# Regrouping the fetch of edge slots in a graph layer, and moving its evictions and splits between two engines

## The chip, the cores and the metric

One core of one Trainium2 chip runs the whole kernel as one program. The metric is the device time in microseconds (us) of one execution, and the time of a kernel is the median over several executions.

## The reference

The kernel computes two rounds of message passing with a gated recurrent cell, on 12,500 nodes with 64 features and 400,000 edges. The edges come sorted by `dst`; the sum goes by `src` (the reference names it `row`).

```python
h = jnp.maximum(_layernorm(x, axis=-1), 0.0)
for t in range(2):
    m_input = jnp.concatenate([h[dst], h[src], edge_weight1], axis=1)
    messages = m_input @ msg_W[t].T + msg_b[t]
    agg = jax.ops.segment_sum(messages, src, num_segments=12500)
    h = _gru_cell(agg, h, gru_Wih[t], gru_bih[t], gru_Whh[t], gru_bhh[t])
return x + h
```

## The kernel before, in words

The nodes lie in 98 tiles of 128 (`NT`). The edges are cut into 112 windows (`C`), one to a partition, 3572 edges each. The program goes through four parts.

1. Loading and packing, to about 100 us. Each edge is packed into two 32-bit words that hold the source node, the place of the destination in its window, and the bits of the edge's weight (`attr`).
2. A sort of each window's words by source tile, to about 600 us. VectorE (DVE in the profile) does the merge steps, ScalarE (ACT) copies, layer norm and counts beside them.
3. The spreading block (lines 831 to 950), from 600 to about 719 us. For each window and each node tile it takes the 64 slots in which the edges of that tile lie. It is the part that the change rewrites.
4. Two rounds (`sums_round`, line 969), 720 to 1563 us and 1574 to 2399 us. TensorE (PE) gathers rows of `h` with one-hot matrices from VectorE, ScalarE evicts them, TensorE scatters them into sums per node, and the gate arithmetic follows two tiles behind.

The spreading block goes by groups of tiles, given by the table `GROUPS` at line 787: tiles 0 to 23, 24 to 47, 48 to 71 and 72 to 97.

- SyncE stores the sorted words to memory (L834). Then GpSimd (POOL) issues 49 indirect fetches (L848), each for a pair of tiles, into `taken`. They are all in one queue and wait for nothing but the sorted words. Each group has a semaphore of its own, `taken_in[g]`.
- VectorE waits for its group (L903) and decodes it in seven passes, one after the other: the lane of the destination (L920), the source tile's place (L922 and L927 or L929), the two pieces of the weight (L930, L931, L933), and their sum (L934, which raises `src_ready`). All seven cover the 112 windows and all slots of the group: 64 elements for each tile. Where the group crosses the middle of the tiles (`MID`), the subtraction is in two instructions. In the last group a check of the slots' ends comes first (L908 to L914).
- TensorE turns the decoded slots, four tiles to a pack (L862 for the source lanes, L863 for the weights), into two banks each of PSUM, so that pack k waits until pack k-2 has been evicted.
- ScalarE evicts the source lanes (L881, two halves of each pack) into `src_lane`, and VectorE evicts the weights (L941) into `attr_slot`.
- At the end of a group the weights are split into a 16-bit high part and a 16-bit rest scaled by 2048: ScalarE makes the high part (L888), VectorE subtracts it (L945), ScalarE scales the rest (L890) and writes the high part beside it (L892). VectorE's next group comes behind L945.
- ScalarE also converts the destination lanes (L874), which SyncE stores to memory (L838) for the rounds.
- After the last group come a short check (L947, L948, L868, L950), whose result `misfit` every engine reads before the rounds.

At the start of a round VectorE clears two small buffers (L1346, L1349) and the whole of `rows` (L1351); in round 0 it then writes ones into one column (L1354). Only then comes its first one-hot matrix (L1284), which needs the lanes that were fetched from memory (L1017, issued by GpSimd in round 0 and by SyncE in round 1). TensorE and ScalarE wait for `rows_zero` before their first instruction of a round. In round 0 a row of `rows` has 132 elements of 16 bits: 128 features that ScalarE writes (L1200), two that VectorE writes (L1289), the ones, and a last one. In round 1 it has 128, all written by ScalarE.

Of the kernel before, what the change touches and what calls it, by code (L numbers as in the profile page):

```python
# [130 lines left out]
def build(nc, x, src, dst, attr, msg_W, msg_b, Wih, bih, Whh, bhh, out):  # L131
    N, H = x.shape
    E = src.shape[0]
    ROUNDS = msg_W.shape[0]
    NT = -(-N // P)
# [3 lines left out]
    C = 112  # L139
# [6 lines left out]
    J = -(-C // 2)  # L146
# [22 lines left out]
    with ExitStack() as ctx:  # L169
# [12 lines left out]
        def sem(name):  # L182
            return ctx.enter_context(nc.semaphore(name))
# [3 lines left out]
        def path_sem(name):  # L187


            if name not in path_sems:  # L190
                path_sems[name] = sem(name)
            return path_sems[name]
# [19 lines left out]
        h = sb("h", [P, NT, HA])  # L212
# [574 lines left out]
        GROUPS = [range(4 * (a * -(-NT // 4) // 4), min(4 * ((a + 1) * -(-NT // 4) // 4), NT)) for a in range(4)]  # L787
# [33 lines left out]
        high_cut = sem("high_cut")  # L821
        low_left = sem("low_left")
        low_cut = sem("low_cut")
# [7 lines left out]
        with nc.Block() as block:  # L831
# [39 lines left out]
            def _(act):  # L871
                for g, group in enumerate(GROUPS):
# [12 lines left out]
                    at = slice(group[0], group[-1] + 1)  # L885
                    act.wait_ge(attr_kept, 2 * (group[-1] // 4 + 1))
                    wait(act, low_left, g)
                    nc.scalar.activation(attr_high[:, 0:len(group), :], attr_slot[:, at, :], ACT.Copy).then_inc(high_cut, 1)  # L888
                    act.wait_ge(low_left, g + 1)
                    nc.scalar.activation(attr_two[:, at, :, 1], attr_slot[:, at, :], ACT.Copy, scale=LO).then_inc(low_cut, 1)  # L890
                    act.wait_ge(low_cut, g + 1)
                    nc.scalar.activation(attr_two[:, at, :, 0], attr_high[:, 0:len(group), :], ACT.Copy)  # L892

            @block.vector
            def _(dve):
# [5 lines left out]
                for g, group in enumerate(GROUPS):  # L901
# [34 lines left out]
                    for k, pack in enumerate(PACKS):  # L936
                        if pack[0] not in group:
                            continue
                        dve.wait_ge(slots_ps, k + 1)
                        for half in range(2):  # L940
                            nc.vector.tensor_copy(attr_slot[half * SLOTS:(half + 1) * SLOTS, pack[0]:pack[-1] + 1, :],  # L941
                                                  ps_attr[k % 2][0:SLOTS, 0:len(pack) * C]
                                                  .rearrange("p (s j h) -> p s j h", j=J, h=2)[:, :, :, half]).then_inc(attr_kept, 1)
                    dve.wait_ge(high_cut, g + 1)
                    nc.vector.tensor_tensor(attr_slot[:, at, :], attr_slot[:, at, :], attr_high[:, 0:n, :], ALU.subtract).then_inc(low_left, 1)  # L945
# [23 lines left out]
        def sums_round(r, scope):  # L969
# [18 lines left out]
            else:  # L988
# [13 lines left out]
             rz_ready, tn_ready, cand_ready, mixed, h_new, ones_ready, joined_ready) = [path_sem(f"{n}_{r}") if more or n not in ("attr_sum", "ones_ready") else None for n in names]  # L1002
# [22 lines left out]
            with nc.Block() as block:  # L1025
# [87 lines left out]
                def _(te):  # L1113
# [57 lines left out]
                    te.wait_ge(rows_zero, 1)  # L1171
# [22 lines left out]
                def _(act):  # L1194
# [46 lines left out]
                    act.wait_ge(rows_zero, 1)  # L1241
# [37 lines left out]
                def _(dve):  # L1279
# [71 lines left out]
                    nc.vector.memset(rows[:], 0.0).then_inc(rows_zero, 1)  # L1351
                    if r == 0:
                        dve.wait_ge(rows_zero, 1)
                        nc.vector.memset(rows[:, :, :, 2 * H + 2:2 * H + 3], 1.0).then_inc(ones_ready, 1)  # L1354
                        dve.wait_ge(ones_ready, 1)
# [297 lines left out]
```

## Time and profile before

| what | value |
|---|---|
| runs | 2413.81 us median of 3 (2413.45 to 2416.66) |
| the profiled execution's own time | 2400.32 us |
| its span, first to last instruction | 2398.8 us |
| spreading block and start of round 0 | 599.84 to 725.12 us |
| VectorE busy | 2192.0 us, 91% |
| ScalarE busy | 1963.7 us, 82% |
| TensorE busy | 1621.8 us, 68%; granted clock 0.979 |
| GpSimd busy | 612.9 us, 26% |

The span runs from the first to the last instruction of the profiled execution, and its own time is 1.5 us longer. Times of rows are in microseconds from the start of the span. A row of the timeline gives start, duration, engine, line, operation, output and inputs, and in brackets how long the engine had been idle before it and what ended that. Consecutive instructions of the same kind are merged into one row (x2, x4). Busy times do not say what bounds a stretch; for that the waits at each place are read.

### The profile page before, as it was taken

What the parts mean: (1) busy time and instruction counts of PE and PEld (TensorE: products, weight loads), DVE (VectorE), ACT (ScalarE), POOL (GpSimd) and SP (SyncE); (2) the same over time, 40 slices, a digit from 0 to 9 for tenths busy, and PEclk for the clock granted to TensorE, in tenths of its full rate; (3) what the DMA queues carried; (4) which work ended last, traced back from release to release, by engine and by line L of the source; (5) the groups of instructions that cost most, each with busy time, mean ns of one, the idle gap of its engine ahead of it and who ended that gap; (6) DMA issues with size and microseconds to landing.
All of it is one profiled execution on the core that took longest, in us unless ns stands there. A gap on an engine that the chain in (4) does not pass through costs nothing. (4 is left out here: it accounts for less than half of the span.)

```text
span 2398.8 us, 126601 instructions
## 1 busy us (share of the span) xinstructions
PE 1621.8 (68%) x47260; PEld 1529.0 (64%) x47260; DVE 2192.0 (91%) x3766; ACT 1963.7 (82%) x4390; POOL 612.9 (26%) x853
## 2 busy tenths in 40 slices
PE   0000000000138899999999999968999999999996
PEld 0000000000138899999999999858999999999996
DVE  6999999999369899999999999868999999999995
ACT  3776895563158899999999999868999999999996
POOL 1000000000633344454554444401211111211121
PEclk9999999999968999999999999989999999999998
DMA  5100001110426666666666666556766777677773
GB/s 105 41 0 0 0 0 38 45 22 21 124 49 228 211 226 224 232 228 227 227 228 227 226 231 225 176 193 202 238 235 233 243 233 239 235 243 233 237 237 116
DMA packets 175418, 400.70 MB, mean 167 GB/s; under 512 B 73071, under 2 KB 76789, under 8 KB 174855
## 3 DMA queue, kind: packets, MB, share of 16 engines
q1 hardware_dynamic: 116907, 204.17, 27.0%
q0 software_dynamic: 57296, 195.19, 24.4%
q8 instruction: 49, 0.80, 0.1%
q10 hardware_dynamic: 1132, 0.27, 0.1%
q14 instruction: 34, 0.28, 0.0%
HBM read 384.63 MB, written 14.57 MB: 166 GB/s over the span
## 5 line engine op out<-in xcount | busy, mean ns | idle before, releaser
L1200 ACT ACTIVATE rows<-ps_rows 128x512 f16<-128x512 f32 x2744 | 1454.4, 637 | 66.9 <-PE ps_rows L1123 44.3
L1140 PE MATMUL ps_sum<-rows,src 128*64 128x132 f16 (+1 forms) x21952 | 1153.3, 225 | 15.0 <-ACT rows L1200 9.4
L1140 PEld LDWEIGHTS ps_sum<-rows,src 128*64 128x64 f16 x21952 | 905.1, 142 | 26.8 <-ACT rows L1200 18.6
L1293 DVE TENSOR_TENSOR src<-iota_units,src_lane 128x2048 f16<-128x2048 f16 (+1 forms) x784 | 863.3, 1101 | 42.7 <-PE ps_sum L1140 42.6
L1123 PE MATMUL ps_rows<-rows_next,dst 128*64 128x128 f16 x10976 | 547.9, 220 | 37.2 <-DVE dst L1284 22.3
L1123 PE MATMUL ps_rows<-rows_now,dst 128*64 128x128 f16 x10976 | 546.1, 220 | 22.2 <-DVE dst L1284 10.3
L1284 DVE TENSOR_SCALAR dst<-lanes,lane_no 128x2048 f16<-128x2048 f16 (+1 forms) x784 | 533.0, 680 | 4.2 <-DMA lanes<-lanes_dram 3.6
L862 PE MATMUL ps_src<-ident,late 112*64 112x112 f32 x98 | 29.9, 337 | 627.0 <-DVE taken L934 626.4
L1123 PEld LDWEIGHTS ps_rows<-rows_next,dst 128*64 128x64 f16 x10976 | 413.0, 111 | 60.4 <-issue 26.9
L1123 PEld LDWEIGHTS ps_rows<-rows_now,dst 128*64 128x64 f16 x10976 | 412.9, 111 | 45.3 <-issue 15.9
L862 PEld LDWEIGHTS ps_src<-ident,late 112*64 112x64 f32 x98 | 14.6, 149 | 629.7 <-DVE taken L934 627.3
L1017 POOL DMA_DIRECT2D lanes<-lanes_dram x392 | 242.5, 619 | 467.5 <-DVE dst L1284 400.9
L1052 POOL COPY copied<-h 128x64 f32 (+1 forms) x196 | 173.5, 886 | 606.3 <-PE ps_T L1155 596.9
L848 POOL DMA_INDIRECT taken<-sorted_dram,start_i x49 | 58.3, 1189 | 571.7 <-DMA sorted_dram<-planes 557.1
L291 ACT ACTIVATE beyond<-src_i,below 128x3572 bf16<-128x3572 int32 x49 | 159.7, 3260 | 24.4 <-issue 20.2
L1165 PE MATMUL ps_gates<-w_first,turned_now 128*64 128x256 f32 x784 | 119.6, 381 | 5.9 <-ACT turned_now L1214 3.3
L1167 PE MATMUL ps_gates<-w_second,turned_now 128*64 128x256 f32 x784 | 118.9, 379 | 0.0
L1214 ACT ACTIVATE turned_now<-ps_T 128x256 f32<-128x256 f32 x196 | 77.6, 396 | 4.9 <-PE ps_T L1155 4.9
L1289 DVE COPY rows<-attr_room 128x32 f16 (+3 forms) x392 | 74.1, 189 | 7.7 <-PE ps_sum L1140 7.6
L1153 PE MATMUL ps_T<-ident,copied 128*64 128x128 f32 x392 | 76.2, 276 | 0.0
L1152 PE MATMUL ps_T<-ident,joined 128*64 128x128 f32 x392 | 76.1, 276 | 0.0
L1167 PEld LDWEIGHTS ps_gates<-w_second,turned_now 128*64 128x64 f32 x784 | 57.6, 137 | 27.2
(188 smaller groups left out, 2052.6 us busy)
## 6 DMA issues: line engine op xcount, KB each, us to landing
lanes<-lanes_dram POOLq DMA_DIRECT2D x294, 512.0 KB, 4.8
lanes<-lanes_dram SPq DMA_DIRECT2D x294, 512.0 KB, 4.7
lanes<-lanes_dram POOLq DMA_DIRECT2D x98, 256.0 KB, 4.1
lanes<-lanes_dram SPq DMA_DIRECT2D x98, 256.0 KB, 4.1
rows_now<-parts_dram SPq DMA_DIRECT2D x112, 32.0 KB, 1.7
rows_next<-parts_dram SPq DMA_DIRECT2D x112, 32.0 KB, 3.6
parts_dram<-rows_now SPq DMA_DIRECT2D x1, 3136.0 KB, 16.2
sorted_dram<-planes SPq DMA_DIRECT2D x1, 3136.0 KB, 11.6
```

What stands on the lines that cost most here:

```text
L291: nc.scalar.activation(beyond[:], src_i[:], ACT.Sign, bias=below[:, m:m + 1], accum_out=balance[:, m:m + 1]).then_inc(counts_ready, 1)
L1017: plain(engine.dma_start(lanes[q][:, 0:n * SLOTS], lanes_dram[bass.ds(s, 1), q * QC * SLOTS:(q * QC + n) * SLOTS] .broadcast_to([P, n * SL ...
L1052: plain(nc.gpsimd.tensor_copy(copied[b][:], h[:, bass.ds(k, 1), 0:H].rearrange("p o f -> p (o f)"))).then_inc(copied_ready, 1)
L1123: last = nc.tensor.matmul(ps_rows[(u + NU * b) % 4][half * SLOTS:(half + 1) * SLOTS, k * 2 * H:(k + 1) * 2 * H], dst1[q][:, (c - q * QC) * ...
L1140: last = nc.tensor.matmul(ps_sum[b][at, 0:width], hot[:, at], row, start=(j == 0), stop=(j == J - 1))
L1153: nc.tensor.matmul(ps_T[high, 0:P], copied[b][:], ident[:], start=True, stop=True)
L1165: nc.tensor.matmul(ps_gates[at, to], turned_now[b][:, at], w_first[:, r, :], start=True, stop=False)
L1167: last = nc.tensor.matmul(ps_gates[at, to], turned_now[b][:, P + at.start:P + at.stop], w_second[:, r, :], start=False, stop=True)
L1200: nc.scalar.activation(rows[:, (u + NU * b) % ring, 0:n, 0:2 * H], cut(ps_rows[(u + NU * b) % 4][:])[:, 0:n, :], ACT.Copy).then_inc(rows_r ...
L1214: nc.scalar.activation(turned_now[b][:], ps_T[:, 0:2 * P], ACT.Copy).then_inc(T_ready, 1)
L1284: nc.vector.tensor_scalar(dst1[q][:, 0:n * SLOTS], lanes[q][:, 0:n * SLOTS], lane_no[:, 0:1], None, ALU.is_equal).then_inc(dst1_ready, 1)
L1293: nc.vector.tensor_tensor(src1[q][:, 0:len(units)], iota_units[:].rearrange("p (o l) k -> p o l k", o=1) .broadcast_to([P, len(units), P, ...
```

## The change

The groups become 32, 28, 20 and 18 tiles. ScalarE evicts both halves of a pack, source lanes and weights. The split of the weights is now four instructions of VectorE alone (L937 to L940 in the changed kernel), and it stands one group later: after the decode of group g+1 VectorE splits group g. In the rounds, only columns 130 and 131 of `rows` are zeroed in round 0, and nothing in round 1; the waits for `rows_zero` are left in round 0 alone.

```diff
-        GROUPS = [range(4 * (a * -(-NT // 4) // 4), min(4 * ((a + 1) * -(-NT // 4) // 4), NT)) for a in range(4)]
+        ENDS = [0, *(4 * (NT * part // (4 * 49)) for part in (16, 30, 40)), NT]
+        GROUPS = [range(ENDS[a], ENDS[a + 1]) for a in range(4)]
...
-                    at = slice(group[0], group[-1] + 1)
-                    act.wait_ge(attr_kept, 2 * (group[-1] // 4 + 1))
-                    wait(act, low_left, g)
-                    nc.scalar.activation(attr_high[:, 0:len(group), :], attr_slot[:, at, :], ACT.Copy).then_inc(high_cut, 1)
-                    act.wait_ge(low_left, g + 1)
-                    nc.scalar.activation(attr_two[:, at, :, 1], attr_slot[:, at, :], ACT.Copy, scale=LO).then_inc(low_cut, 1)
-                    act.wait_ge(low_cut, g + 1)
-                    nc.scalar.activation(attr_two[:, at, :, 0], attr_high[:, 0:len(group), :], ACT.Copy)
+                        for half in range(2):
+                            nc.scalar.activation(attr_slot[half * SLOTS:(half + 1) * SLOTS, pack[0]:pack[-1] + 1, :],
+                                                 ps_attr[k % 2][0:SLOTS, 0:len(pack) * C]
+                                                 .rearrange("p (s j h) -> p s j h", j=J, h=2)[:, :, :, half],
+                                                 ACT.Copy).then_inc(attr_kept, 1)
...
-                    for k, pack in enumerate(PACKS):
-                        if pack[0] not in group:
-                            continue
-                        dve.wait_ge(slots_ps, k + 1)
-                        for half in range(2):
-                            nc.vector.tensor_copy(attr_slot[half * SLOTS:(half + 1) * SLOTS, pack[0]:pack[-1] + 1, :],
...
-                    dve.wait_ge(high_cut, g + 1)
-                    nc.vector.tensor_tensor(attr_slot[:, at, :], attr_slot[:, at, :], attr_high[:, 0:n, :], ALU.subtract).then_inc(low_left, 1)
+                def split_attr(g):
+                    n, at = len(GROUPS[g]), slice(GROUPS[g][0], GROUPS[g][-1] + 1)
+                    dve.wait_ge(attr_kept, 2 * -(-(GROUPS[g][-1] + 1) // 4))
+                    step(nc.vector.tensor_copy(attr_high[:, 0:n, :], attr_slot[:, at, :]))
+                    step(nc.vector.tensor_tensor(attr_slot[:, at, :], attr_slot[:, at, :], attr_high[:, 0:n, :], ALU.subtract))
+                    step(nc.vector.tensor_scalar(attr_two[:, at, :, 1], attr_slot[:, at, :], LO, None, ALU.mult))
+                    step(nc.vector.tensor_copy(attr_two[:, at, :, 0], attr_high[:, 0:n, :]))
+
+                decode(0)
+                for g in range(1, len(GROUPS)):
+                    decode(g)
+                    split_attr(g - 1)
+                split_attr(len(GROUPS) - 1)
...
-                    te.wait_ge(rows_zero, 1)
+                    if r == 0:
+                        te.wait_ge(rows_zero, 1)
...
-                    nc.vector.memset(rows[:], 0.0).then_inc(rows_zero, 1)
                     if r == 0:
+                        nc.vector.memset(rows[:, :, :, 2 * H + 2:width], 0.0).then_inc(rows_zero, 1)
                         dve.wait_ge(rows_zero, 1)
```

`decode(g)` is the body of the old loop over the groups, from the wait for the fetch to L934.

The order on VectorE, at the end of one decode and through the next. Before, group 0 (`late` and `taken` are the decoded words, `ps_attr` the turned weights, `attr_room` holds `attr_slot` and `attr_two`):

```order
L927 TENSOR_TENSOR late<-tile_base,late 112x1536
L930 TENSOR_SCALAR taken<-taken 112x12x128
L931 TENSOR_SCALAR taken<-taken 112x12x128
L933 TENSOR_SCALAR taken<-taken,units 112x12x128
L934 SCALAR_TENSOR_TENSOR taken<-taken,units 112x12x128
L941 COPY attr_room<-ps_attr 64x224 x12
L945 TENSOR_TENSOR attr_room<-attr_room,late 128x1344
L920 TENSOR_SCALAR late<-taken 112x1536
```

With the change, from the end of the decode of group 0 to the split of its weights:

```order
L930 SCALAR_TENSOR_TENSOR taken<-taken,units 112x16x128
L916 TENSOR_SCALAR late<-taken 112x1792
L918 TENSOR_SCALAR late<-taken 112x1792
L923 TENSOR_TENSOR late<-tile_base,late 112x1152
L925 TENSOR_TENSOR late<-late,tile_base 112x640
L926 TENSOR_SCALAR taken<-taken 112x14x128
L927 TENSOR_SCALAR taken<-taken 112x14x128
L929 TENSOR_SCALAR taken<-taken,units 112x14x128
L930 SCALAR_TENSOR_TENSOR taken<-taken,units 112x14x128
L937 CAST late<-attr_room 128x1792
L938 TENSOR_TENSOR attr_room<-attr_room,late 128x1792
L939 TENSOR_SCALAR attr_room<-attr_room 128x1792
```

The evictions have left VectorE, the next decode follows at once, and the split of the older group comes behind it.

The same engine at the end of the block. Before:

```order
L934 SCALAR_TENSOR_TENSOR taken<-taken,units 112x13x128
L941 COPY attr_room<-ps_attr 64x224 x12
L941 COPY attr_room<-ps_attr 64x112 x2
L945 TENSOR_TENSOR attr_room<-attr_room,late 128x1456
L947 TENSOR_REDUCE over<-ps_check 6x1
```

With the change:

```order
L929 TENSOR_SCALAR taken<-taken,units 112x9x128
L930 SCALAR_TENSOR_TENSOR taken<-taken,units 112x9x128
L937 CAST late<-attr_room 128x1120
L938 TENSOR_TENSOR attr_room<-attr_room,late 128x1120
L939 TENSOR_SCALAR attr_room<-attr_room 128x1120
L940 COPY attr_room<-late 128x1120
L937 CAST late<-attr_room 128x1008
L938 TENSOR_TENSOR attr_room<-attr_room,late 128x1008
L939 TENSOR_SCALAR attr_room<-attr_room 128x1008
L940 COPY attr_room<-late 128x1008
L948 TENSOR_REDUCE over<-ps_check 6x1
```

Two splits stand behind the last decode now, that of group 2 and that of group 3, and the check behind them.

ScalarE in the last group. Before:

```order
L874 ACTIVATE planes<-late 112x1664
L881 ACTIVATE src_lane<-ps_src 64x224 x12
L881 ACTIVATE src_lane<-ps_src 64x112 x2
L888 ACTIVATE late<-attr_room 128x1456
L890 ACTIVATE attr_room<-attr_room 128x1456
L892 ACTIVATE attr_room<-late 128x1456
```

With the change:

```order
L872 ACTIVATE planes<-late 112x1152
L879 ACTIVATE src_lane<-ps_src 64x224 x2
L884 ACTIVATE attr_room<-ps_attr 64x224 x2
...
L879 ACTIVATE src_lane<-ps_src 64x112 x2
L884 ACTIVATE attr_room<-ps_attr 64x112 x2
L829 UNCONDITIONAL_BRANCH
```

ScalarE has four evictions for each pack, and nothing behind the last pack.

## Rows read from the trace of the kernel before

**Rows 1.** Timeline of VectorE, group 0.
```profile
629.74 0.96 DVE L920 TENSOR_SCALAR late<-taken 112x1536 int32<-112x1536 int32 x1 [29.20 <-DMA taken<-sorted_dram,start_i]
...
634.40 0.96 DVE L931 TENSOR_SCALAR taken<-taken 112x1536 int32<-112x1536 int32 x1
...
636.46 1.82 DVE L934 SCALAR_TENSOR_TENSOR taken<-taken,units 112x1536 f32<-112x1536 int32 x1
...
648.06 1.56 DVE L945 TENSOR_TENSOR attr_room<-attr_room,late 128x1344 f32<-128x1344 f32 x1 [1.39 <-ACT late L888]
```

**Rows 2.** Timeline of GpSimd: fetches; below, landing after their start, 684 to 685.
```profile
626.22 0.92 POOL L848 DMA_INDIRECT taken<-sorted_dram,start_i  x1 [0.30 <-issue]
...
629.90 1.78 POOL L848 DMA_INDIRECT taken<-sorted_dram,start_i  x1 [0.30 <-issue]
631.99 2.49 POOL L848 DMA_INDIRECT taken<-sorted_dram,start_i  x1 [0.30 <-issue]
...
636.84 2.23 POOL L848 DMA_INDIRECT taken<-sorted_dram,start_i  x1 [0.30 <-issue]
...
641.83 0.93 POOL L848 DMA_INDIRECT taken<-sorted_dram,start_i  x1 [0.30 <-issue]
...
684.41 0.93 POOL L848 DMA_INDIRECT taken<-sorted_dram,start_i  x1 [0.30 <-issue]
...
DMA to landing us min/median/max: 2.6/2.7/2.7
```

**Rows 3.** Timeline of VectorE, the last group and the check.
```profile
690.07 0.24 DVE L908 TENSOR_SCALAR planes<-taken 112x98 int32<-112x98 int32 x1
...
691.79 1.88 DVE L920 TENSOR_SCALAR late<-taken 112x1664 int32<-112x1664 int32 x1
...
697.42 1.09 DVE L930 TENSOR_SCALAR taken<-taken 112x1664 int32<-112x1664 int32 x1
...
713.44 1.67 DVE L945 TENSOR_TENSOR attr_room<-attr_room,late 128x1456 f32<-128x1456 f32 x1 [1.48 <-ACT late L888]
...
715.76 0.15 DVE L950 TENSOR_SCALAR misfit<-ps_check 1x1 int32<-1x1 f32 x1 [0.28 <-PE ps_check L868]
```

**Rows 4.** Timeline of TensorE, first turned tiles of groups 0 and 3.
```profile
638.33 0.39 PE L862 MATMUL ps_src<-ident,late 112*64 112x112 f32 x1 [585.09 <-DVE taken L934]
...
702.88 0.39 PE L862 MATMUL ps_src<-ident,late 112*64 112x112 f32 x1 [16.52 <-DVE taken L934]
```

**Rows 5.** Timeline of ScalarE, first eviction, four in a row, and the block's end.
```profile
640.07 0.72 ACT L881 ACTIVATE src_lane<-ps_src 64x224 f16<-64x224 f32 x2 [7.85 <-PE ps_attr L863]
...
664.08 1.49 ACT L881 ACTIVATE src_lane<-ps_src 64x224 f16<-64x224 f32 x4 [0.52 <-PE ps_attr L863]
...
716.99 1.82 ACT L892 ACTIVATE attr_room<-late 128x1456 f16<-128x1456 f16 x1
```

**Rows 6.** Groups by shape, a conversion while loading: busy us, mean ns, idle us before.
```profile
L413 DVE CAST iota_units<-src_lane 128x512 f16<-128x512 int32 x1 | 0.4, 421 | 0.0
```

**Rows 7.** Groups by shape, 629 to 716 us: evictions by VectorE.
```profile
L941 DVE COPY attr_room<-ps_attr 64x224 f32<-64x224 f32 x48 | 18.4, 383 | 16.1 <-PE ps_attr L863 15.0
```

**Rows 8.** Timeline and landing time of the first fetch of lanes, start of round 0.
```profile
720.14 0.19 DVE L1346 MEMSET extras<- 128x64 f32 x2 [4.24 <-issue]
...
720.51 2.22 POOL L1017 DMA_DIRECT2D lanes<-lanes_dram  x4 [35.17 <-issue]
721.32 3.14 DVE L1351 MEMSET rows<- 128x3696 uint32 x1 [0.85 <-DVE extras L1349]
725.12 0.75 DVE L1284 TENSOR_SCALAR dst<-lanes,lane_no 128x2048 f16<-128x2048 f16 x1 [0.29 <-DMA lanes<-lanes_dram]
...
DMA to landing us min/median/max: 4.5/4.5/4.5
```

**Rows 9.** Timeline of VectorE, start of round 1.
```profile
1574.50 0.91 DVE L1351 MEMSET rows<- 128x1024 uint32 x1 [0.30 <-DVE extras L1349]
1577.94 0.75 DVE L1284 TENSOR_SCALAR dst<-lanes,lane_no 128x2048 f16<-128x2048 f16 x1 [2.53 <-DMA lanes<-lanes_dram]
```

More of the change, by code:

```diff
@@ L820, in build @@
         attr_kept = sem("attr_kept")
-        high_cut = sem("high_cut")
-        low_left = sem("low_left")
-        low_cut = sem("low_cut")
         lanes_out = sem("lanes_out")
@@ L900, in _, with decode @@
                 step(nc.vector.tensor_copy(check[:, 1:5], stray[:]))
-                for g, group in enumerate(GROUPS):
+                def decode(g):
+                    group = GROUPS[g]
                     n, at = len(group), slice(group[0], group[-1] + 1)
@@ L935, in _ @@
                                                    op0=ALU.mult, op1=ALU.add).then_inc(src_ready, 1)
-                    for k, pack in enumerate(PACKS):
-                        if pack[0] not in group:
-                            continue
-                        dve.wait_ge(slots_ps, k + 1)
-                        for half in range(2):
-                            nc.vector.tensor_copy(attr_slot[half * SLOTS:(half + 1) * SLOTS, pack[0]:pack[-1] + 1, :],
-                                                  ps_attr[k % 2][0:SLOTS, 0:len(pack) * C]
-                                                  .rearrange("p (s j h) -> p s j h", j=J, h=2)[:, :, :, half]).then_inc(attr_kept, 1)
-                    dve.wait_ge(high_cut, g + 1)
-                    nc.vector.tensor_tensor(attr_slot[:, at, :], attr_slot[:, at, :], attr_high[:, 0:n, :], ALU.subtract).then_inc(low_left, 1)
+                def split_attr(g):
[10 more added lines that the diff above has]
+                split_attr(len(GROUPS) - 1)
                 dve.wait_ge(check_ps, 1)
@@ L1001, in sums_round @@
              extras_zero, extras_ready, scaled_ready, copied_ready, turned, T_ready, gates_ready,
-             rz_ready, tn_ready, cand_ready, mixed, h_new, ones_ready, joined_ready) = [path_sem(f"{n}_{r}") if more or n not in ("attr_sum", "ones_ready") else None for n in names]
+             rz_ready, tn_ready, cand_ready, mixed, h_new, ones_ready, joined_ready) = [path_sem(f"{n}_{r}") if more or n not in ("attr_sum", "ones_ready", "rows_zero") else None for n in names]
             lanes_in = [path_sem(f"lanes_in{r}_{q}") for q in range(NQ)]
@@ L1239, in tanhs @@
                         nc.scalar.activation(cand[:], tn[:], ACT.Tanh).then_inc(cand_ready, 1)
-                    act.wait_ge(rows_zero, 1)
+                    if r == 0:
+                        act.wait_ge(rows_zero, 1)
                     def body(s, b, half):
```

## The prediction

> **What bounds the kernel now.** I read the page first: VectorE is busiest, but the edit touches only 600 to 725 us and the start of each round, so shares over the whole span say nothing about it. The timelines of that stretch, engine by engine, do. In group 0 VectorE starts when its fetches have landed, decodes from 629.74 [rows 1] until TensorE starts at 638.33 [rows 4], 8.59 us, and evicts. It then waits 1.39 us for ScalarE and subtracts at 648.06 [rows 1]. The later groups follow directly: their fetches have landed by the time VectorE asks. The last fetch starts at 684.41 [rows 2], and VectorE opens the last group at 690.07 [rows 3]. So before, VectorE's chain with its two partners is the bound. The block ends with ScalarE's last copy, 716.99 + 1.82 = 718.81 [rows 5], and round 0 begins 1.33 us later, at 720.14 [rows 8].
>
> GpSimd is the second chain, 2 us in hand. Alone, a fetch takes 0.92 us and the next comes 1.23 us after it. In this decode fetches take 1.78, 2.49 and 2.23 us, under evictions out of PSUM again 0.93 [rows 2]. The slow ones end at joints of VectorE's work: the one from 631.99 ends at 634.48, where L931 starts at 634.40, and the one from 636.84 ends at 639.07, 0.79 us after the sum L934 ended at 638.28 [rows 1, 2]. A fetch passes two gates: its start waits behind any of the seven passes, its end only behind the passes at two elements a cycle.
>
> **The parts, priced.**
>
> *First group.* 16 fetches instead of 12. The 15th starts at 629.90, the 16th 1.23 later at 631.13; from start to VectorE takes 3.52 us (626.22 to 629.74) [rows 1, 2]: decode 0 starts at 634.65, 4.9 us later than before. The last fetches landed 2.7 us after their start [rows 2]; if those on which VectorE waits do too, each wait ends 0.75 us earlier, which I keep as a bound.
>
> *Decodes.* A pass at two elements a cycle costs 0.96 us for 1536 elements [rows 1] and 0.42 for 512 [rows 6]: 0.067 us for each pair of tiles (128 elements). At one a cycle it is 1.56 us for 1344, so 0.133 a pair. Five of one and two of the other make 0.60 a pair: 11.0 us for 16 pairs, 9.8 + 0.2 for 14 (the subtraction is in two), 7.4 for 10. The last group has 9 pairs, an odd number, and the nearest row is the old last group of 13. There L920 took 1.88 us where twelve pairs took 0.96, and L930 took 1.09 [rows 3]; the four slow passes lose 0.133 a pair, the three in place 0.27 altogether: 702.88 - 691.79 = 11.09 [rows 3, 4] less 2.1 less 0.8 is 8.2 us. The check ahead of it costs 1.72 (690.07 to 691.79). Were L920 slow for another reason than the odd count, the last decode would be 1.2 us cheaper.
>
> The Trainium skill says why the count should matter (VectorE: DVE Perf Modes, What auto-detection actually checks): two elements a cycle from one source need outermost dimensions of source and destination that are both even or equal. By that rule nine pairs are slow again in L916 and L918; without it the end is 1.2 us earlier.
>
> *Splits.* Not in the trace as VectorE work. Nearest: the conversion of 512 at 0.42 us [rows 6] and the subtraction [rows 1]. For 1792, 1568, 1120 and 1008 weights that gives 5.4, 4.9, 3.7 and 3.4 us; at one element a cycle for three of the passes the last would be 5.0. I take the first, since nothing here reads PSUM.
>
> *Evictions.* VectorE's took 383 ns [rows 7]; four on ScalarE are 1.49 us, 373 ns each [rows 5]. That is TensorE's own pace for a pack at the start of a group (640.07 + 1.49). So four and a half packs take 1.74 us to the first eviction, then 4 x 1.49 + 1.1, and 0.3 where TensorE waits for a bank: 9.1 us. If a 32-bit output costs more, 0.5 us for each 0.1 us a pack.
>
> [...]
>
> *The fetch queue.* This decides. I step the 33 remaining fetches along VectorE's new order by the two gates. Stepped so along the old order, they end within 1.3 us of the last row. While decode 0 runs (to 645.65), GpSimd gets through three and a half; alone again it ends the 30th at 656.4, and group 1 opens at 659.0. VectorE has idled 13 us there, since split 0 stands behind decode 1 and cannot fill it. Decode 1 and split 0 run to 674.4 and hold the fetches back again; the 40th ends at 676.6, group 2 opens at 679.2. Decode 2 and split 1 run to 691.5, the 49th fetch starts at 692.6, 8.2 us later than before, and group 3 opens at 696.1.
>
> *The tail.* 696.1 + 1.7 + 8.2 = 706.0. Split 2 lies beside the evictions, which end at 715.1. Split 3 ends at 718.5, the check takes 0.8 more (713.44 + 1.67 to 715.76 + 0.15 [rows 3]), and 1.33 later round 0 begins: 720.6 to 720.9, against 720.14. **Block: +0.6 us.** VectorE's chain loses its evictions, 12 x 0.38 = 4.6 us a group [rows 7] and the waits between them, and gets them back as waits for fetches.
>
> *The clearing.* It removes 3.14 us in round 0 and 0.91 in round 1. But lanes fetched at 720.51 land 4.5 us later, at 725.0, and VectorE's first one-hot starts at 725.12 [rows 8]: the clearing ended just as they landed. Without it VectorE waits for the lanes, worth 0.1 us; at most 0.3 more if the landing gets shorter. In round 1 VectorE waits 2.53 us for lanes after the clearing [rows 9]: nothing. TensorE and ScalarE wait for the one-hots anyway. **-0.1 us.**
>
> Sum: +0.5 us on the profiled execution's 2400.3. That execution is 0.6% under the median of the runs, so I carry the ratio: 2413.8 + 0.5 = **2414.3 us**. Bounds of the open prices: landing 0.75 earlier, the odd count 1.2 earlier, the gates 1 each way, new passes that hold no fetch 2 earlier, evictions and split 3 slower 2 to 3 later. They will not all fall on one side: -4 to +4 us.
>
> **Rivals.** About 0.2%, 4.8 us, is what a measurement of this kernel can tell from no change.
>
> 1. *The fetches are not held.* At 1.23 us each the last would start at 671.7, the decodes would come when VectorE is ready (decode 1 at 651.9, decode 2 at 667.3), the last would end near 689.6, and round 0 would begin near 704: 16 us less, 2398 us. For it: larger passes leave fewer joints but also fewer interruptions. Against it: all three rows under the decode are 1.78 or more [rows 2]. 8%.
> 2. *Slower: fetches miss the joints.* Passes follow within 0.04 us, and the splits lengthen the bursts behind decodes 1 and 2. If no fetch gets through under a split, four more fetches queue: 4 x 1.23 = 4.9 us later, 2419. If none gets through in any burst (11.0, 15.4 and 12.3 us), the last starts near 710, 18 us later, 2432. It decides from the fourth missed fetch on. Against it: four got through in each old decode. 10%.
> 3. *The clearing counts in full*: 4.0 us off, 2410, within 0.2%. Against it are the two waits for lanes. 4%.
> 4. *The same chain, cheaper*: splits at 32 bits or with 16-bit outputs do not hold the fetches (2 us) and the landing is early (0.75): 2411 to 2413. For it: no row shows a pass with a 16-bit output beside a fetch. Against it: the decode's passes of the same kind did. 12%.
>
> The Trainium skill (SBUF — State Buffer, Who interferes with whom) says that a VectorE instruction in a two-port mode shuts GpSimd out for the whole instruction, and one with two SBUF inputs only its reads. Of this change it says beware: the splits are put where fetches are issued. Taken instruction by instruction it gives my walk; taken for a whole burst, rival 2.
>
> **How the numbers follow.** The forecast holds 66%, rivals 4 and 3 fall within 0.2% too. Faster by over 0.2%: 8% and 1 for an unseen one, 9%. Slower: 10%. Within: 81%. The range 2409 to 2420 takes in the bounds and the near end of rival 2.
>
> **What would show it.** In the new trace: decode 0 opens near 634.7; VectorE idles some 13, 5 and 5 us ahead of decodes 1, 2 and 3, each ended by the fetch; the last fetch starts near 692.6; L916 takes about 1.35 us in the last group; split 3 starts about 9 us behind the last decode; round 0's first one-hot waits 3 to 4 us for lanes and starts near 725.6. If the last fetch starts before 688 or after 697, the walk is wrong; if decodes 1 to 3 open without idling, rival 1 is right; if one-hots start 2 us or more ahead of 725, rival 3.

## The result, and the profile after

| | kernel before | changed kernel |
|---|---|---|
| runs beside each other, median | 2413.63 us (8 runs, 2406.81 to 2420.17) | 2402.03 us (8 runs, 2394.16 to 2406.0) |
| profiled execution: its own time, span | 2400.32, 2398.8 us | 2394.16, 2392.5 us |
| granted TensorE clock, mean | 0.979 | 0.981 |
| ratio, 95% interval | | 0.9949 [0.9931, 0.9967] |

So the change is 0.5% faster, about 12 us, where no change was forecast (+0.5 us). The two profiled executions are only 6.2 us apart, half of that; where the rest lies turned out to be the lesson of this case.

The changed kernel's spans must be read with an offset. Its spreading stretch starts, at own_start, at 596.04 us; in the kernel before at 599.87. I call the time from own_start to round 0's first one-hot **the stretch**: 725.12 - 599.87 = 125.25 us before, 718.60 - 596.04 = 122.56 after. VectorE in the stretch, from the timeline of the changed kernel (start, us, engine, line, operation, in brackets the idle time before it and what ended it):

```profile
596.04 0.15 DVE L892 TENSOR_SCALAR own_start<-lane_no 128x1 f32<-128x1 f32 x1 [0.33 <-PEq L596]
...
630.16 1.23 DVE L916 TENSOR_SCALAR late<-taken 112x2048 int32<-112x2048 int32 x1 [33.44 <-DMA taken<-sorted_dram,start_i]
...
638.74 2.35 DVE L930 SCALAR_TENSOR_TENSOR taken<-taken,units 112x2048 f32<-112x2048 int32 x1
653.53 1.09 DVE L916 TENSOR_SCALAR late<-taken 112x1792 int32<-112x1792 int32 x1 [12.44 <-DMA taken<-sorted_dram,start_i]
...
663.38 1.09 DVE L937 CAST late<-attr_room 128x1792 f16<-128x1792 f32 x1
...
672.83 0.83 DVE L916 TENSOR_SCALAR late<-taken 112x1280 int32<-112x1280 int32 x1 [3.83 <-DMA taken<-sorted_dram,start_i]
...
689.17 0.25 DVE L904 TENSOR_SCALAR planes<-taken 112x98 int32<-112x98 int32 x1 [4.11 <-DMA taken<-sorted_dram,start_i]
...
690.90 1.34 DVE L916 TENSOR_SCALAR late<-taken 112x1152 int32<-112x1152 int32 x1
...
697.58 1.42 DVE L930 SCALAR_TENSOR_TENSOR taken<-taken,units 112x1152 f32<-112x1152 int32 x1
...
707.99 0.69 DVE L937 CAST late<-attr_room 128x1008 f16<-128x1008 f32 x1 [5.31 <-ACT attr_room L884]
...
713.92 0.18 DVE L1349 MEMSET extras<- 128x64 f32 x2 [1.58 <-issue]
...
718.60 0.75 DVE L1287 TENSOR_SCALAR dst<-lanes,lane_no 128x2048 f16<-128x2048 f16 x1 [3.75 <-DMA lanes<-lanes_dram]
```

The reader is to see the three new waits for the fetch, 12.44, 3.83 and 4.11 us, where VectorE had none [rows 3]; the last group, 689.17 to 699.00, in place of a decode of 13 pairs; split 3 waiting for ScalarE; and the one-hot waiting 3.75 us for its lanes where it started on time before [rows 8]. The fetches, from GpSimd's timeline of the changed kernel, the answer to [rows 2]:

```profile
627.36 0.93 POOL L846 DMA_INDIRECT taken<-sorted_dram,start_i  x1 [0.30 <-issue]
...
629.83 1.67 POOL L846 DMA_INDIRECT taken<-sorted_dram,start_i  x1 [0.30 <-issue]
631.81 1.52 POOL L846 DMA_INDIRECT taken<-sorted_dram,start_i  x1 [0.31 <-issue]
633.63 2.60 POOL L846 DMA_INDIRECT taken<-sorted_dram,start_i  x1 [0.30 <-issue]
```

The first of these is the 16th fetch, the other three are the 18th to the 20th. Alone a fetch takes 0.93 us; under decode 0 they are held, as forecast (a fetch is held when it takes longer because VectorE is at work). And VectorE opens at 630.16, 2.80 us after the start of the 16th fetch at 627.36, not 3.52.

ScalarE now evicts both kinds. Its timeline in group 0 of the changed kernel:

```profile
647.38 0.72 ACT L879 ACTIVATE src_lane<-ps_src 64x224 f16<-64x224 f32 x2
648.13 0.72 ACT L884 ACTIVATE attr_room<-ps_attr 64x224 f32<-64x224 f32 x2
650.64 0.72 ACT L879 ACTIVATE src_lane<-ps_src 64x224 f16<-64x224 f32 x2 [1.79 <-PE ps_attr L861]
...
656.31 0.72 ACT L879 ACTIVATE src_lane<-ps_src 64x224 f16<-64x224 f32 x2 [4.20 <-remote]
...
659.90 0.72 ACT L879 ACTIVATE src_lane<-ps_src 64x224 f16<-64x224 f32 x2 [2.12 <-PE ps_attr L861]
...
662.89 1.70 ACT L872 ACTIVATE planes<-late 112x1792 f16<-112x1792 int32 x1
```

The pace is 1.50 us a pack, as priced. But packs 5, 6 and 7 (650.64, 656.31, 659.90) come 1.8, 4.2 and 2.1 us late from TensorE, 8 us together. No row of the kernel before had such a gap, and I first took it for harmless: VectorE waits for fetches until 653.53, decode 1 needs no eviction, and split 0 asks for them only at 663.38, when they have just ended.

### The profile page after: what moved, and what is told of

Same layout as the page of the kernel before. It is cut to its first block and busy times, and to the rows that moved or that the text cites. A ratio compares the mean times of both kernels' runs of the same rounds, so it can differ in the third digit from the quotient of the medians.

```text
span 2392.5 us, 126600 instructions
## 1 busy us (share of the span) xinstructions
PE 1623.6 (68%) x47260; PEld 1526.9 (64%) x47260; DVE 2179.6 (91%) x3727; ACT 1963.7 (82%) x4428; POOL 616.3 (26%) x853
## 5 line engine op out<-in xcount | busy, mean ns | idle before, releaser
L846 POOL DMA_INDIRECT taken<-sorted_dram,start_i x49 | 63.8, 1302 | 571.7 <-DMA sorted_dram<-planes 557.1
## 6 DMA issues: line engine op xcount, KB each, us to landing
sorted_dram<-planes SPq DMA_DIRECT2D x1, 3136.0 KB, 11.6
```

## The experiments

Every series of executions ran the kernel before on the same chip beside the kernels under test. The single time of a program spreads by about 0.7%, so I read two numbers of each: the ratio, and the stretch in the trace. The walk, below, is the one of the prediction: the fetches stepped one after the other along VectorE's order of work.

**Repeats.** No edit: the kernel before and the changed kernel once more. Theories at this point: *A*, the edit gains on VectorE's chain in the stretch; *B*, chance or loading (the first VectorE operation that needs a bias, L433, started at 27.53 us against 31.38, which accounts for 3.85 of the 6.2 us).

> The kernel before, unchanged, timed against itself. It tells how far the ratio of two equal kernels strays, and gives a second trace of the old program. Theory A (the gain is what the two traces show between the start of the spreading block and the first one-hot, 125.25 against 122.56 us, and the rest is chance from execution to execution): ratio 1.000 within its interval, that stretch again 125.3 us within 0.5, while the weights' addition L433, which started at 31.38 us before and at 27.53 with the change, may start anywhere between. Theory B (the changed program as a whole is placed or loaded differently, and gains outside the stretch too): L433 again at 31.4 here.

> The changed kernel again, unchanged. Theory A: stretch from own_start to the first one-hot 122.6 us within 0.5, that is 2.7 us less than before, and a ratio of about 0.999; L433 anywhere between 27 and 32 us. Theory B: ratio again near 0.995, L433 again at 27.5 us.

Measured, in one series: before_twice 0.9996 [0.9979, 1.0014], stretch 124.79 us; after_twice 0.9987 [0.9972, 1.0003], stretch 122.96. The stretch repeats within 0.5 us; the 0.5% does not. The two later repeats of the changed kernel:

> The changed kernel a third time, unaltered. Theory A (2.3 to 2.7 us of real gain in the spreading stretch): ratio 0.9985 to 0.999, stretch 122.6 to 123.2 us. Theory D (the first measured 0.9949 is what the edit does and the second was a bad draw): ratio 0.996 or less. Theory B (the loading is faster for this kernel's placement, 4 to 6 us): L433 starts near 25 to 28 us again, where the kernels with other code started it at 31 to 33; if it starts at 30 or more, that difference was chance.

> The changed kernel a fourth time, unaltered, beside the kernel before on a chip of its own choosing. Theory A (the real gain is the 2.3 us of the stretch): ratio 0.9983 to 0.999, stretch 122.6 to 123.0. Theory D (0.9949 is what the edit does on some chips): 0.996 or less here.

after_thrice 0.9983 [0.9969, 0.9997], stretch 122.84, L433 at 31.41; after_fourth **0.9927** [0.9912, 0.9942], stretch 122.34, L433 at 25.18. The medians of the changed kernel hardly move (2402.0, 2400.9, 2402.4, 2400.9 us); the kernel before beside it had 2413.6, 2404.2, 2407.9 and 2418.8. It is the old kernel that differs from series to series. And L433 is chance: in two traces of the same kernel (VectorE's timeline of before_thrice)

```profile
24.21 0.42 DVE L433 TENSOR_TENSOR w_node<-w_node,bias 66x256 f32<-66x256 f32 x1 [0.17 <-ACT w_node L397]
```

and of before_twice

```profile
30.98 0.42 DVE L433 TENSOR_TENSOR w_node<-w_node,bias 66x256 f32<-66x256 f32 x1 [5.86 <-DMA bias<-in_L_gnn_gru_bhh_dram]
```

it lies 6.8 us apart. Theory B explains a part of the profiled difference. It can't move the medians if the start of L433 is drawn anew in each execution; that it is, I take from the traces of both kernels, where it lies at 24 to 31 us without order.

**One part alone: the clearing.** The kernel before with the new clearing; the waits for `rows_zero` are in round 0 alone, as in the changed kernel (lines not shown).

```diff
-                    nc.vector.memset(rows[:], 0.0).then_inc(rows_zero, 1)
                     if r == 0:
+                        nc.vector.memset(rows[:, :, :, 2 * H + 2:width], 0.0).then_inc(rows_zero, 1)
```

> The kernel before with only the clearing of rows cut down. Prediction's account (the clearing is hidden behind the fetch of lanes): stretch 124.9 to 125.3 us, round 1 unchanged, ratio 1.000. Rival (the clearing counts in executions that are not profiled): 4 us less, ratio 0.998. If the whole gain of 11 us came from here, ratio 0.995.

> Only the clearing changed. Under theory E, where before is at 0.975 here: if the clearing's part is what keeps the clock up, this runs at 0.979 or more and near 2404; if not, at 0.975 and 2419 like the kernel before.

1.0007 [0.9993, 1.002] and 1.0008 [0.999, 1.0025], stretches 126.18 and 126.67 us: no gain. The stretch is even 1 to 2 us longer than the kernel before's, where 124.9 to 125.3 was expected. Some 0.8 us of that is the lanes, which arrive 5.4 and 5.3 us after their fetch is issued instead of 4.6 in the first trace of the kernel before (in clear_only VectorE waits 4.82 us for them); why they are later stays open. The reverse, the changed kernel with the old clearing put back:

> The changed kernel with the whole rows' buffer cleared again. If the clearing is worth nothing (the prediction's term), the stretch from own_start to round 0's first one-hot stays at 122.6 to 123.2, the one-hot's wait for its lanes shrinks from 3.75 us by the 3.14 us of the clearing, and round 1 is the same. If it counts in full, the stretch is 3 us longer, 125.7, and the time 4 us (0.17%) more than the changed kernel's.

0.999 [0.9976, 1.0004], stretch 122.63 (in the same series the changed kernel had 0.9983 [0.9969, 0.9997]). The 3.14 us are back, at 719.28, and the one-hot's wait for its lanes falls to 0.33 (VectorE's timeline of after_old_clear):

```profile
719.28 3.14 DVE L1352 MEMSET rows<- 128x3696 uint32 x1 [0.85 <-DVE extras L1350]
722.68 0.10 DVE L1355 MEMSET rows<- 128x56 f16 x1 [0.26 <-DVE rows L1352]
723.12 0.75 DVE L1285 TENSOR_SCALAR dst<-lanes,lane_no 128x2048 f16<-128x2048 f16 x1 [0.33 <-DMA lanes<-lanes_dram]
```

In the stretch the clearing is worth nothing, in both directions; the ratios show nothing of it either, and can't tell 1 or 2 us.

**The groups alone, and the new division of work alone.** The first is the kernel before with the two lines of ENDS and GROUPS; the second is the changed kernel with the old line of GROUPS and the old clearing.

> Only the groups of the fetch are changed (32, 28, 20 and 18 tiles); VectorE evicts attr as before, and the clearing is the old one. Theory A (what the edit gains it gains on VectorE's chain in the spreading stretch, from own_start to round 0's first one-hot): here VectorE keeps its old chain of decode and evictions, so the smaller last group saves its decode and 8 tiles of eviction, but the first decode comes 4.9 us later; stepped through, the stretch becomes 1.8 us longer than the 125.25 of the kernel before, some 127, and the time changes by no more than 0.1%. Theory B (the gain is chance or lies in the loading): the stretch tells nothing, and the start of L433 lies at 27 rather than 31 us or not without regard to the edit. Theory C (the smaller last group alone is what gains): the stretch becomes 2 us or more shorter, 123.

> New groups, old work. Under theory E, where before is at 0.975 here: 0.979 and 2408 if the groups are what keeps the clock up, 0.975 and 2420 if not. Where before is at 0.979 here: ratio 1.001 as before.

> Evictions on ScalarE, split on VectorE one group later, with the old groups of 24, 24, 24 and 26 tiles and the old clearing. The walk of the fetch queue with landings 1.85 us after a fetch's end: the stretch is 127.1 us, 1.9 longer than before, the last fetch starts about 3 us later than before, VectorE idles about 10, 12 and 13 us ahead of the decodes 1 to 3; ratio 1.001. If the moved work were what gains, the stretch would be 122 to 123 us and the ratio near 0.996.

> Old groups, new division of evictions and splits. Under theory E, where before is at 0.975 here: 0.979 and 2407 if ScalarE's evictions are what keeps the clock up, 0.975 and 2420 if not. Where before is at 0.979 here: ratio 1.001 as in the first series.

groups_only 1.0014 [0.9998, 1.003] and 1.001 [0.9995, 1.0024], stretches 126.27 and 128.11. work_only 1.0012 [0.9995, 1.003] and 1.0009 [0.9992, 1.0025], stretches 128.16 and 127.35. Alone, each makes the stretch 1.4 to 3.3 us longer than the 124.9 us that the three traces of the kernel before without late packs have on average; together they make it 2.2 us shorter (122.7). In work_only VectorE waits for the fetch ahead of decodes 1, 2 and 3, and then still has the old last group with 26 tiles to evict (its timeline):

```profile
648.65 0.96 DVE L915 TENSOR_SCALAR late<-taken 112x1536 int32<-112x1536 int32 x1 [9.99 <-DMA taken<-sorted_dram,start_i]
...
668.98 0.96 DVE L915 TENSOR_SCALAR late<-taken 112x1536 int32<-112x1536 int32 x1 [7.52 <-DMA taken<-sorted_dram,start_i]
...
690.71 0.24 DVE L903 TENSOR_SCALAR planes<-taken 112x98 int32<-112x98 int32 x1 [8.72 <-DMA taken<-sorted_dram,start_i]
...
715.73 0.92 DVE L936 CAST late<-attr_room 128x1456 f16<-128x1456 f32 x1 [7.98 <-ACT attr_room L883]
```

Taking the evictions away makes the fetch the bound; the uneven groups then cut what lies behind the last fetch.

**Is the fetch chain what decides?** Split 1 behind decode 3 instead of behind decode 2; the work is the same:

```diff
                 for g in range(1, len(GROUPS)):
                     decode(g)
-                    split_attr(g - 1)
-                split_attr(len(GROUPS) - 1)
+                    if g != 2:
+                        split_attr(g - 1 if g == 1 else 1)
+                split_attr(2)
+                split_attr(3)
```

> The changed kernel with split 1 behind decode 3 instead of behind decode 2; the work is the same. Theory A, with the fetch queue as the chain that decides: under split 1 the fetches of group 3 are held, so without it the last fetch ends 2.4 us earlier, decode 3 opens 2.4 us earlier, splits 1 and 2 lie beside the last evictions (8.6 us of 9.1), and the stretch is 2.4 us shorter than the changed kernel's, some 120.3 us. Rival (VectorE's own work sets the end): moving a split changes nothing or makes the end later by what no longer fits beside the evictions, up to 1 us.

0.9982 [0.9966, 0.9998], stretch 119.82: 3.0 us shorter than the changed kernel's in the same series, 2.4 expected. (The two ratios, 0.9982 and 0.9983, can't tell the two kernels apart; the medians are 2.0 us apart.) The last fetch starts 87.53 us behind own_start (688.33 - 600.80) instead of 90.04, and splits 1 and 2 fit beside the evictions (split 3 waits 0.29 us for ScalarE). A split under the fetches costs; the rival falls.

**Other groups.** The third number of ENDS is 42 in last14; 16, 32, 44 with the late split 1 in last10_late; 12, 28, 40 in first24.

> The changed kernel with groups of 32, 28, 24 and 14 tiles. Theory A with the walk along the fetch queue: the last fetch ends 0.6 us later, decode and evictions of the last group are shorter by 3.5 us, stretch 119.9 us (2.9 less than the changed kernel's 122.8), ratio to the kernel before 0.997. Rival (the fetch queue is held for longer behind the larger group 2): no more than 1 us shorter, 122.

> Groups of 32, 28, 24 and 14 tiles a second time. From the first run's stretch of 120.16 us, 4.9 less than the kernel before: ratio 0.998 where the kernel before is at 0.979, 0.991 where it is at 0.975; stretch 120.0 to 120.4 us.

> Groups of 32, 32, 24 and 10 tiles, and split 1 behind decode 3. By the walk the stretch is 4.9 us shorter than the changed kernel's, 117.9 us, which is 7 us (0.3%) less than the kernel before: ratio 0.997. Rival: the splits 1 and 2 (9.8 us) no longer fit beside the evictions of ten tiles, and split 3 starts late: 119.5 to 120 us, no better than split_late alone.

> The changed kernel with groups of 24, 32, 24 and 18 tiles, so that VectorE waits on the 12th fetch and not on the 16th. It tells what the first landing hangs on: in four kernels with a first group of 24 tiles VectorE opened 2.6 to 2.7 us behind the end of the 12th fetch, in five with 32 tiles 1.8 to 1.9 behind the 16th. If it is the place in the queue, 2.6 to 2.7 here; if it was the rest of the old kernel, 1.9. The stretch: 0.6 us longer than the changed kernel's by the walk (a smaller group 0 only moves the holds), 123.4; if decode 0 five microseconds earlier counted in full, 118.

last14: **0.9907** [0.9891, 0.9922] and 0.991 [0.9888, 0.9931], stretches 120.16 and 120.23; walk right within 0.3 us. In its first series its median is 3.1 us under the changed kernel's (2397.77 against 2400.85), where the intervals of the two ratios still overlap; the stretch is 2.1 to 2.8 shorter than in every trace of the changed kernel. Its medians, 2397.8 and 2397.1 us, are the lowest of all; but split1_late and last10_late have stretches as short, and split1_late never ran beside it. last10_late: 0.9917 [0.9901, 0.9933], stretch 119.78, two us more than the walk said: here the rival was right, split 3 follows split 2 without a wait. first24: 0.9926 [0.991, 0.9941], stretch 121.50, where the walk said 123.4: it missed by 1.9 us, and why is not shown. The 12th fetch, 620.77 to 621.69 on GpSimd's timeline, and the decode on VectorE's of first24:

```profile
620.77 0.92 POOL L846 DMA_INDIRECT taken<-sorted_dram,start_i  x1 [0.30 <-issue]
...
624.47 0.97 DVE L916 TENSOR_SCALAR late<-taken 112x1536 int32<-112x1536 int32 x1 [29.36 <-DMA taken<-sorted_dram,start_i]
```

are 2.78 us apart, from the end of the one to the start of the other. So the long first landing goes with the 12th place in the queue, not with the rest of the old kernel. What is special at that place, the last section shows.

**Where the old kernel loses more.** after_fourth and the first series left 12 to 18 us, of which the stretch in the traces explained 2.2. The mean granted clock of the kernel before was 0.9754 in the series of after_fourth and 0.979 in the quiet ones, the changed kernel's 0.981 to 0.982 in all: so some place should be longer, with TensorE at half clock. I repeated the kernel before until a trace of it showed the place.

> The kernel before, unaltered. In two series of executions it took 2404 and 2408 us at a mean granted clock of 0.979, in a third 2419 at 0.975, where the changed kernel took 2401 to 2403 at 0.981 to 0.982 in all of them. Theory E: there are two behaviours of this program's clock, one with some 20 us more at half clock; if this series shows the second, the trace has that half-clock time in one place inside a round or at a round's start, and the profiled time is near 2415. Theory F (drift of the chip, no matter which program): all kernels here move together.

2401.71 us, 0.9992 [0.9978, 1.0005], clock 0.979, stretch 124.61: the quiet behaviour again.

> The kernel before, unaltered, once more. Three series gave it 2404, 2406 and 2408 us at a mean granted clock of 0.979, two gave 2414 and 2419. If this one shows 0.975, its trace is to show where the extra half-clock time lies (theory E: one place); if it shows 0.979 the time is 2402 to 2408 and its stretch 124.8 to 125.3 us, and where the slower series spend the extra time stays open.

2413.6 us, beside 2420.64 for the same text, both at a mean clock of 0.976, ratio 0.9976 [0.9961, 0.9991]; and the stretch of its profiled execution is **138.99 us**, 14 more than in the other three traces of it (124.61 to 125.25). The rest of the program is not longer (round 0, from its first one-hot to VectorE's last instruction in it, 835.4 us, 837.6 in the first trace). VectorE's timeline of before_fourth:

```profile
625.98 0.96 DVE L920 TENSOR_SCALAR late<-taken 112x1536 int32<-112x1536 int32 x1 [29.40 <-DMA taken<-sorted_dram,start_i]
...
638.97 1.68 DVE L941 COPY attr_room<-ps_attr 64x224 f32<-64x224 f32 x4 [0.37 <-PE ps_attr L863]
643.42 0.80 DVE L941 COPY attr_room<-ps_attr 64x224 f32<-64x224 f32 x2 [2.78 <-remote]
648.45 0.80 DVE L941 COPY attr_room<-ps_attr 64x224 f32<-64x224 f32 x2 [4.24 <-remote]
650.64 1.56 DVE L945 TENSOR_TENSOR attr_room<-attr_room,late 128x1344 f32<-128x1344 f32 x1 [1.39 <-issue]
652.12 0.95 DVE L920 TENSOR_SCALAR late<-taken 112x1536 int32<-112x1536 int32 x1
...
677.37 0.80 DVE L941 COPY attr_room<-ps_attr 64x224 f32<-64x224 f32 x2 [6.27 <-remote]
...
681.03 0.95 DVE L920 TENSOR_SCALAR late<-taken 112x1536 int32<-112x1536 int32 x1
```

The same places in before_thrice:

```profile
638.78 1.63 DVE L941 COPY attr_room<-ps_attr 64x224 f32<-64x224 f32 x4 [0.28 <-PE ps_attr L863]
641.79 1.56 DVE L945 TENSOR_TENSOR attr_room<-attr_room,late 128x1344 f32<-128x1344 f32 x1 [1.39 <-ACT late L888]
643.27 0.95 DVE L920 TENSOR_SCALAR late<-taken 112x1536 int32<-112x1536 int32 x1
...
663.10 0.95 DVE L920 TENSOR_SCALAR late<-taken 112x1536 int32<-112x1536 int32 x1
```

Packs 5, 6 and 12 come 2.8, 4.2 and 6.3 us late, packs 10 and 11 some 1.1 and 1.9 us. From decode 0 to decode 1 it is 26.14 us instead of 19.34 (643.27 - 623.93), from decode 1 to decode 2 28.91 instead of 19.83: 15.9 us, of which 1.7 come back later, where the fetches have long landed (the last one starts at 675.28). Busy time by windows of before_fourth (window, its length, busy us and instructions of TensorE, its weight loads, VectorE, ScalarE and GpSimd, then TensorE's granted clock, the transfers' share and GB/s):

```profile
640.00:680.00 40.00, 9.24 (x64) 8.10 (x63) 17.01 (x27) 13.54 (x23) 28.28 (x27) 0.65 0.36 89
680.00:720.00 40.00, 13.32 (x95) 11.86 (x96) 31.51 (x46) 18.53 (x29) 0.00 (x0) 0.62 0.12 18
720.00:760.00 40.00, 24.16 (x678) 23.09 (x678) 31.77 (x67) 28.03 (x53) 12.90 (x19) 0.79 0.56 188
```

and of before_thrice:

```profile
720.00:760.00 40.00, 36.62 (x1060) 35.05 (x1058) 36.27 (x78) 35.73 (x74) 16.25 (x25) 0.94 0.72 234
```

Through the block the granted clock goes back and forth between half and full, 0.62 to 0.65 on average; it stays up only when round 0 loads TensorE, and here that is later. So I read the low mean clock as a consequence of the stall. The size fits: 14 us at half clock in 2410 would take 0.979 down to 0.976 (an estimate from these figures).

Packs 5 and 6 are just those that are late in the changed kernel's first trace. They are late in every trace of the series in which the old kernel is slow (after, after_fourth, last14, last14_twice, last10_late, first24, before_fourth) and in none of the twelve other traces taken in the quiet series, nor in the first trace of the kernel before. In the changed kernel the wait falls into the 12.4 us in which VectorE idles for group 1, and into decode 1 behind them. ScalarE's timeline of after_fourth,

```profile
655.86 0.72 ACT L879 ACTIVATE src_lane<-ps_src 64x224 f16<-64x224 f32 x2 [4.89 <-remote]
...
661.76 1.70 ACT L872 ACTIVATE planes<-late 112x1792 f16<-112x1792 int32 x1
```

ends group 0's evictions 66.8 us behind own_start (594.97), that of after_thrice without late packs (own_start 599.89)

```profile
655.96 0.72 ACT L879 ACTIVATE src_lane<-ps_src 64x224 f16<-64x224 f32 x2
...
658.96 1.70 ACT L872 ACTIVATE planes<-late 112x1792 f16<-112x1792 int32 x1
```

59.1 us: 7.7 us of lateness, and yet the stretches are 122.34 and 122.84. So the changed kernel is not merely shorter by 2.2 us, it absorbs this lateness, for which the old one pays 6.8 us between decodes 0 and 1. The second lateness of before_fourth, at packs 10 to 12, costs the old kernel 9.1 us more; in the changed kernel's two traces with late packs it does not occur at all, and why not is open. The stall of the one trace and the 2.2 us make 16 us, between the 12 and the 18 of the two series.

## Why the prediction was wrong

**The step that failed: the base of the sum.** "That execution is 0.6% under the median of the runs, so I carry the ratio." The profiled execution took 2400.3 us and the runs 2413.45 to 2416.66. That 13 us is not a scale factor. It has the size of the stall found in before_fourth (14 us in the stretch), in the very block that the change rewrites. The trace I argued from was without it. So the sum added the change's effect to a time that the runs don't have, and put at nothing what the change does to the other 13 us: measured, the medians came 11.6 us down. Carried as an unknown term, it would have been asked where the change could touch it, and the range's low end would have been 2414 - 13 - 3. That the runs of the first series had the stall is inferred, from the old kernel's median and from the late packs in the changed kernel's trace there; it is seen directly only in before_fourth. And in the series of before_fourth two kernels of one text were 0.24% apart, so that not all of the 0.5% need be the change's.

**The term that was mis-sized: the landing**, in the part on the first group and in the fetch queue. I took 3.52 us from a fetch's start to VectorE, from the one wait there was [rows 1, 2], and kept 0.75 earlier for each wait as a bound. The changed kernel's four waits end 2.80, 2.70, 2.76 and 3.05 us after the fetch's start: the landing column's 2.7 [rows 2] was the right row. Four waits in one chain add up, 0.72 + 0.82 + 0.76 + 0.47 = 2.8 us: idles of 12.44, 3.83 and 4.11 where "13, 5, 5" stood. With 2.8 off, "720.6 to 720.9" is 717.8 to 718.1 on the old kernel's clock; it began at 713.92 + 3.83 = 717.75. "Block: +0.6 us" was -2.4. In the quiet series the ratios were 0.9987 [0.9972, 1.0003] and 0.9983 [0.9969, 0.9997], with which 2.2 us (0.9991) agrees; "within 0.2%" would have held there. The row with 3.52 us is itself a special one: a load of instructions lies in that landing (last section).

Point by point, on the old kernel's clock (3.83 us added):
- *First group*: decode 0 opens at 633.99, not 634.65; the landing again.
- *Decodes*: 10.9, 9.9, 7.3 and 8.1 us against 11.0, 10.0, 7.4, 8.2. (The "0.27 altogether" of the odd group is what each of the three passes in place loses over four pairs; the 0.8 in the sum is right.) L916 takes 1.34 us in the last group for 1152 elements where 2048 take 1.23: the odd count costs what I took. The rule of the Trainium skill (VectorE: DVE Perf Modes, What auto-detection actually checks) agrees with both rows.
- *Splits*: 5.6, 5.0, 3.8 and 3.5 us against 5.4, 4.9, 3.7, 3.4. *Evictions* in the last group 8.9 (699.00 to 707.90) against 9.1. The 32-bit output costs nothing extra: 0.72 us for two, like the 16-bit one, and less than VectorE's 0.80 for two in before_fourth. And split 3 starts 9.0 us behind the last decode, as said.
- *The fetch queue*: the last fetch starts at 689.95, not 692.6, inside the bounds of 688 to 697; 2.65 early, of which the first three landings make 2.3. The rest is holding: under decode 0 fetches take 1.52 to 2.77 us, and four of them end there, where "three and a half" stood. The Trainium skill (SBUF — State Buffer, Who interferes with whom) has a two-port instruction shut GpSimd out throughout; the fetches end at joints of such bursts here, so per instruction it agrees.
- *The clearing*: "-0.1 us" was right, and after_old_clear agrees. But my sign for rival 3, one-hots two us ahead of 725, came true (722.43) by another cause. A sign that another term of one's own can produce tells nothing.
- *Rivals*: 1 and 2 fell, since VectorE idled and the fetches met the joints. 4 had the early landing but only once, not once for each wait; its other half, splits that hold no fetch, fell: two fetches that met split 0 took 2.83 and 2.33 us. 3 fell. (The chances as stated add up to 101%.) None of them asked what else might differ between the profiled execution and the runs.

## What to carry to other kernels

If the profiled execution lies outside the spread of the timed runs, the gap may be a term with a place in the program: look for it before scaling, or widen the range by it on the side on which the change gives slack. A chain that waits on a transfer takes the landing once per wait, so take it from the column over many rows. And a producer's engine with idle time behind its consumers can be worth more than its mean gain, since it swallows stalls: here the change was worth 2.2 us of the stretch in quiet series (3 to 6 us between the medians, within the noise of that) and 12 to 18 us in the others.

## What the runs showed of the hardware that I had not expected

- TensorE's answers came late by 2 to 6 us at the same packs in three of the six series, and in the other three not at all. The series ran on different chips at different times, which is not separated. In before_fourth the profile's records have TensorE's matmuls of pack 6 at the usual time, and nothing after them until group 1 (timeline of TensorE):

```profile
641.46 0.26 PE L863 MATMUL ps_attr<-ident,taken 112*64 112x112 f32 x1
660.70 0.40 PE L862 MATMUL ps_src<-ident,late 112*64 112x112 f32 x1 [18.98 <-DVE taken L934]
```

  yet VectorE and ScalarE both start on pack 6 only at 648.45. The granted clock was 1.00 from 639 to 645 us. No load of instructions falls between 640 and 650 in the record of the transfers. What holds the answer stays open; nothing was tried against it alone, nor was it tried whether the new division of work without the new groups would absorb it.
- Two kernels of the same text were 7 us apart in one series (0.9976 [0.9961, 0.9991]) where this stall occurs, and equal (0.9996, 0.9992) where it does not.
- A fetch that VectorE waited for landed 1.8 to 2.1 us after its end at most places, but 2.6 to 2.8 at the 12th, in each of the nine traces that wait there. It is not the place alone: the 40th of first24 took 2.75 us and the 36th of work_only_twice 2.91. In all eleven the record of the transfers has one load of instructions that starts 0.4 to 1.5 us after the fetch's end. Transfers in the first trace of the kernel before, 627.14 to 629.74 us, and in first24, 666.54 to 669.29 (queue, packets, MB, share of the transfer engines' time):

```profile
q14 instruction: 1, 0.01, 0.7%
...
q8 instruction: 1, 0.02, 2.2%
```

  In the changed kernels the load behind the 12th fetch is there too, but nobody waits for that fetch. The waits without a load took at most 1.94 us, with one exception: the last fetch of last10_late took 3.4 us, while the store of the lanes (336 KB) ran from 688.9 to 691.9 beside it. Four other waits had a load at that distance and took 1.85 to 2.11 us, so a load alone does not settle it. Nothing was tried against it.
